# Reordering one stage of a fused two-block kernel: products, halves and second norm

## The chip, the cores and the metric

One core of one Trainium2 chip runs the whole program. The metric is device time in microseconds (us), the median of several executions. Five engines work side by side: TensorE (PE in the profile, PEld for its weight loads), VectorE (DVE), ScalarE (ACT), GpSimd (POOL) and SyncE (SP, which here only issues DMAs). Each engine takes its instructions strictly in the order written; they meet at semaphores.

## The reference, cut to what matters

The input is 16 sequences of 512 tokens and 128 features. Two blocks follow each other, and each normalises its input and adds the outputs of two branches to the unnormalised input:

```python
xn = layernorm(x);  x1 = x + scan_block(xn) + experts(xn)        # block 0
x1n = layernorm(x1); out = x1 + level_attention(x1n) + gated_cell(x1n)
# scan_block:  xi,z = split(xn@W_in); B,C = (xi@W_xp)@W_B, ..@W_C; h_t = a_t*h_(t-1) + B*xi
#              y = (C*h + D*xi) * silu(z);  return y @ W_out
# level_attention: W[t,s] = (Q_t.K_s) * decay(t,s) * lam[t, level(t,s)], lower triangle
#              o = (W@V) @ Wout.T + x;   return layernorm(o)*ln_g + ln_b
# gated_cell:  c = sigmoid(f)*c + sigmoid(i)*tanh(g) over the 16 rows; out = tanh(x@wo + c@uo + bo)
```

## The kernel before

Time is cut into 17 stages. Stage (i, j) runs block 1 of sequence i and block 0 of sequence j = i + 1 interleaved; the first has only j = 0, the last only i = 15, and 14 of the stages (i = 1 to 14) are one hardware loop body. In a stage every engine has a list of its own, `stages(i, j)`, written out by hand: its order is the whole schedule. Sequence i is cut into four tiles of 128 tokens (n = 0 to 3) and the tiles into chunks of 32.

The attention of a tile is computed in two parts. Inside a chunk, `pair_scores(i, n)` (TensorE, line 544) makes Q.K into the PSUM bank P1[1]; `pair_levels(i, n)` (line 556) spreads the level weights `nodesT` into P1[2]; VectorE's `pair_weights(i, n)` (lines 1323, 1329, 1333) multiplies the decay in `pair` by the levels, adds `self_lam`, and multiplies by the scores; `chunk_values` (581), `own_heads` (1355) and `chunk_sums` (589) apply it to the values. Across chunks, `left_halves` (TensorE 512 to 516, copied by ScalarE at 918 into `rs`) sums keys and values of left halves, `node_matrices` (530, copied at 928 into `ms`) multiplies them by the head matrices, and `levels`, `level_sum` (1343, 1348) and `tile_sum` (1366) add them up. What feeds them on VectorE: `node_lams` (1256) writes `nodes`, `node_rows` (1265) transposes it into `nodesT`. ScalarE's `pair_decay` (906 and 908) makes the decay from the differences; `own_values` (894) copies values.

Block 0 of sequence j: `scan_c` is the two products with MC (line 394, into P0[2] and P0[0]); the second needs the bank that `scan_inputs` (VectorE 1161) empties, and waits for `bx0_ready`. `scans` (1168, then the products 1173) is the recurrence, `top1` (1126 to 1145) the expert choice, and `gate0` (1178, 1181, 1185) the gating, of which one half stands in tile 0 and one in tile 1.

The second norm belongs to the sequence before: `attention_out(i-1)` (1372) adds the skip, `stats2` and `rstd2` give mean and scale, `norm2(i-1)` (1088, four instructions from `ob` into `skip`) normalises. GpSimd then runs `finish(i-1)` (1546, 1549) into `res`, SP stores `res`, and after that store GpSimd runs `residual(i)` (1499) and `keep_skip(i)` (1541). GpSimd's list per stage is `pair_differences` (1516), `level_values` (1529), `own_level` (1507, writes `self_lam`), `finish(i-1)`, `residual(i)`, `keep_skip(i)`. In the last stage GpSimd, ScalarE and VectorE also run `end_sum`, `end_tanh` and `end_add` for the 16 sequences.

VectorE's middle of a stage before the change reads: `node_lams, scan_inputs, norm2(i-1), node_rows, scans, pair_weights(0), top1, own_heads(0), pair_weights(1), level_sum(0), tile_sum(0), gate0(0), own_heads(1), pair_weights(2), ...`.

Of the kernel before, what the change touches and what calls it, by code (L numbers as in the profile page):

```python
# [23 lines left out]
TILES = T // 128  # L24
# [40 lines left out]
def build(nc, x, weights, consts, out):  # L65
# [9 lines left out]
    with ExitStack() as ctx:  # L75
# [96 lines left out]
        rs = sb("rs", 2048)  # L172
        ms = sb("ms", 2048)
        nodes = ms
        yt, ytT, ob = rs[:, 0:T], rs[:, T:2 * T], rs[:, 2 * T:3 * T]

        tf, ti, tg = ms[:, 0:T], ms[:, T:2 * T], rs[:, 3 * T:4 * T]
        ym = sb("ym", 2 * 512)
# [139 lines left out]
        def _(pe):  # L318
# [73 lines left out]
            def project(j, bank, free, value, lhs, done):  # L392
                pe.wait_ge(R[free], value)
                pe.matmul(P0[bank][:, :], lhs, xnT[:, :], start=True, stop=True).then_inc(R[done], 1)  # L394
# [6 lines left out]
                project(j, 0, "delta_ready", j + 1, MB[:, 0:128], "b0_ps")  # L401
                project(j, 1, "xi0_ready", j + 1, MB[:, 128:256], "b1_ps")

            def scan_c(j):
                project(j, 2, "xi1_ready", j + 1, MC[:, 0:128], "c0_ps")
                project(j, 0, "bx0_ready", j + 1, MC[:, 128:256], "c1_ps")

            def gate_z(j, q):
                if q == 0:
# [212 lines left out]
            def stages(i, j):  # L622
                if j is None:
                    for n in range(3):
                        recurrence(i, j, n)
                if i is not None:
                    heads(i, 0, 4)
                if j is not None:
                    turn_x(j)
                if i is not None:  # L630
                    heads(i, 4, 6)
                    heads(i, 6, 7)
                    running_sums(i)
                    heads(i, 7, 8)
                if j is not None:
                    logits(j)
                if i is not None:
                    left_ends(i)
                    heads(i, 8, 12)
                else:  # L640
                    fold_heads(0, 5)
                if j is not None:
                    scan_x(j)
                else:
                    cell_out()
                if i is not None:
                    heads(i, 12, 14)
                if j is not None:
                    scan_b(j)
                if i is not None:  # L650
                    heads(i, 14, H)
                else:
                    fold_heads(5, 8)
                if j is not None:
                    scan_c(j)
                if i is not None:
                    pair_scores(i, 0)
                    left_halves(i)
                    pair_levels(i, 0)
                    node_matrices(i)  # L660
                    pair_scores(i, 1)
                    chunk_values(i, 0)
                    pair_levels(i, 1)
                    levels(i, 0)
                if j is not None:
                    gate_z(j, 0)
                if i is not None:
                    chunk_sums(i, 0)
                if j is not None:
                    gate_z(j, 1)  # L670
                if i is not None:
                    pair_scores(i, 2)
                    chunk_values(i, 1)
                    pair_levels(i, 2)
                    levels(i, 1)
                if j is not None:
                    gate_u(j, 0)
                if i is not None:
                    chunk_sums(i, 1)
                    pair_scores(i, 3)  # L680
                    chunk_values(i, 2)
                    pair_levels(i, 3)
                    levels(i, 2)
                if j is not None:
                    gate_u(j, 1)
                if i is not None:
                    chunk_sums(i, 2)
                if i is not None:
                    levels(i, 3)
                if j is not None:  # L690
                    out0(j)
                if i is not None:
                    chunk_values(i, 3)
                    if j is not None:
                        recurrence(i, j, 0)
                        recurrence(i, j, 1)
                if j is not None:
                    turn_x1(j)
                if i is not None:
                    chunk_sums(i, 3)  # L700
                    if j is not None:
                        recurrence(i, j, 2)
                    turn_out(i)
                if j is not None:
                    values(j)
                if i is not None:
                    project_out(i)
# [11 lines left out]
        def _(act):  # L719
# [180 lines left out]
                act.wait_ge(R["lev_neg"], i + 1)  # L900
                act.activation(e4[:, :], lev[:, :], ACT.Exp).then_inc(R["e4_ready"], 1)

            def pair_decay(i):

                act.wait_ge(R["diff_ready"], i + 1)
                act.activation(pair[:, :], pair[:, :], ACT.Abs).then_inc(R["diff_abs"], 1)
                act.wait_ge(R["diff_abs"], i + 1)
                act.activation(pair[:, :], pair[:, :], ACT.Exp, scale=-1.0).then_inc(R["decay_ready"], 1)

            def left_halves(i):  # L910
                if later(i):
                    act.wait_ge(R["m_ps"], 4 * i)
                if later(i):
                    act.wait_ge(R["n_ready"], i)
                for n in range(TILES):
                    cols = 384 if n == 3 else 512
                    act.wait_ge(R["r_ps"], 4 * i + n + 1)
                    act.activation(rs[:, 512 * n:512 * n + cols], P1[(3, 4, 0, 3)[n]][:, 0:cols], ACT.Copy)\  # L918
                        .then_inc(R["r_copied"], 1)
# [26 lines left out]
            def stages(i, j):  # L946
# [40 lines left out]
                    fold_heads(5, 8)  # L987
                if i is not None:
                    heads(i, 14, H)
                    pair_decay(i)  # L990
                    own_values(i)
                    left_halves(i)
                    node_matrices(i)
                gelus()
                if j is not None:
# [28 lines left out]
        def _(dve):  # L1024
# [342 lines left out]

            def attention_out(i):
                dve.wait_ge(R["wo_ps"], i + 1)
                if later(i):  # L1370
                    dve.wait_ge(R["n_ready"], i)
                dve.tensor_tensor(ob[:, :], P1[1][:, :], skip[:, :], ALU.add).then_inc(R["ob_ready"], 1)

            def stats2(i):
# [31 lines left out]
            def stages(i, j):  # L1406
# [21 lines left out]
                if i is not None:  # L1428
                    level_weights(i)
                    if later(i):  # L1430
                        stats2(i - 1)
                    node_lams(i)
                if j is not None:
                    scan_inputs(j)
                if i is not None:
                    if later(i):
                        norm2(i - 1)
                    node_rows(i)
                if j is not None:
                    scans(j)  # L1440
                else:
                    cell_out()
                if i is not None:
                    pair_weights(i, 0)
                if j is not None:
                    top1(j)
                if i is not None:
                    own_heads(i, 0)
                    pair_weights(i, 1)
                    level_sum(i, 0)  # L1450
                    tile_sum(i, 0)
                if j is not None:
# [226 lines left out]
```

## Time and profile before

| | |
|---|---|
| median of 3 runs | 1216.23 us (1215.4 to 1220.75) |
| the profiled execution | 1215.93 us, its span 1213.8 us |
| TensorE busy | 1091.7 us, 90% |
| VectorE busy | 1004.4 us, 83% |
| ScalarE busy | 691.8 us, 57% |
| GpSimd busy | 310.4 us, 26% |
| mean granted TensorE clock | 0.959 |

The profiled execution took 2.1 us more than its span; the span runs from the first to the last instruction. A loop stage takes about 71 us and repeats almost exactly, so a stretch of one stage can be read for all. A busy share over the span says which engines could be the bound; which one is, at a given place, is read from who waits there.

### The profile page before, as it was taken

What the parts mean: (1) busy time and instruction counts of PE and PEld (TensorE: products, weight loads), DVE (VectorE), ACT (ScalarE), POOL (GpSimd) and SP (SyncE); (2) the same over time, 40 slices, a digit from 0 to 9 for tenths busy, and PEclk for the clock granted to TensorE, in tenths of its full rate; (3) what the DMA queues carried; (4) which work ended last, traced back from release to release, by engine and by line L of the source; (5) the groups of instructions that cost most, each with busy time, mean ns of one, the idle gap of its engine ahead of it and who ended that gap; (6) DMA issues with size and microseconds to landing.
All of it is one profiled execution on the core that took longest, in us unless ns stands there. A gap on an engine that the chain in (4) does not pass through costs nothing.

```text
span 1213.8 us, 18006 instructions
## 1 busy us (share of the span) xinstructions
PE 1091.7 (90%) x5756; PEld 665.3 (55%) x5756; DVE 1004.4 (83%) x2141; ACT 691.8 (57%) x1366; POOL 310.4 (26%) x197
## 2 busy tenths in 40 slices
PE   5799989998998989899998989989898998989872
PEld 3455646555564655556465555646555564655641
DVE  4688897979979797997979799797979979797677
ACT  4483845738375573837557283755728375572761
POOL 0050320504114050411405041140504114050273
PEclk9899989899999999999899999999999999999885
DMA  3000000000000000000000000000000000001136
GB/s 133 9 9 10 1 18 9 17 9 0 17 9 17 9 17 9 0 17 9 17 9 17 9 0 17 9 17 9 17 9 0 17 9 17 9 17 54 67 101 203
DMA packets 32562, 28.64 MB, mean 24 GB/s; under 512 B 1568, under 2 KB 26144, under 8 KB 32288
## 3 DMA queue, kind: packets, MB, share of 16 engines
q1 hardware_dynamic: 32544, 28.42, 7.2%
q8 instruction: 9, 0.15, 0.0%
q14 instruction: 9, 0.07, 0.0%
HBM read 16.09 MB, written 12.32 MB: 23 GB/s over the span
## 4 chain that ended last, share of the span: by engine, by line
PE 45%; DVE 37%; issue 11%; ACT 5%; DMA 1%; DVEq 0%; ACTq 0%; SPq 0%; POOLq 0%; POOL 0%
DVE ms L1256 6%; PE p L581 4%; PE p L619 3%; DVE skip L1088 3%; PE p L544 3%; PE p L556 2%; PE p L570 2%; DVE pair L1329 2%; DVE nodesT L1265 2%; PE p L433 2%; PE p L394 2%; ACT vdw L849 2%; PE p L424 2%; DVE pair L1323 2%; DVE y L1168 2%
## 5 line engine op out<-in xcount | busy, mean ns | idle before, releaser
L1516 POOL TENSOR_TENSOR pair<-pair,cgt 128x2048 f32<-128x2048 f32 x16 | 58.4, 3647 | 772.5 <-DVE pair L1316 772.5
L858 ACT ACTIVATE gx<-p 128x512 f32<-128x512 f32 x256 | 143.4, 591 | 13.9 <-PE p L479 8.2
L477 PE MATMUL p<-x1Th,Gl 128*128 128x512 f32 x256 | 120.1, 469 | 4.0 <-ACT gx L858 4.0
L813 ACT ACTIVATE gelu<-p,bias_u 128x512 f32<-128x512 f32 x32 | 22.0, 687 | 151.3 <-PE p L424 151.3
L479 PE MATMUL p<-x1Th,Gh 128*128 128x512 f32 x256 | 102.1, 399 | 0.0
L478 PE MATMUL p<-x1Tl,Gh 128*128 128x512 f32 x256 | 101.8, 398 | 0.0
L1529 POOL TENSOR_TENSOR vp<-vdw,beta 128x384 f32<-128x384 f32 (+3 forms) x80 | 80.9, 1042 | 56.0 <-DVE beta L1308 56.0
L544 PE MATMUL p<-gx,x1T 128*32 128x512 f32 x512 | 77.2, 679 | 12.8 <-DVE pair L1333 12.0
L581 PEld LDWEIGHTS p<-vbd,pair 128*128 128x128 f32 x512 | 62.0, 191 | 42.9 <-issue 31.0
L1256 DVE TENSOR_TENSOR ms<-lam,K 128x64 f32<-128x64 f32 (+4 forms) x80 | 84.5, 1132 | 0.0
L394 PE MATMUL p<-xnT,MC 128*128 128x512 f32 x64 | 42.6, 756 | 46.4 <-DVE y L1161 46.4
L581 PE MATMUL p<-vbd,pair 128*128 128x128 f32 x512 | 74.1, 288 | 1.5 <-DVE pair L1333 1.5
L1507 POOL TENSOR_TENSOR self_lam<-lam,K 128x2048 f32<-128x2048 f32 x16 | 75.0, 4689 | 0.0
L819 ACT ACTIVATE sm<-mv 128x4 f32<-128x4 f32 x32 | 6.6, 205 | 117.7 <-DVE mv L1083 117.7
L556 PE MATMUL p<-nodesT,K 128*128 128x512 f32 x128 | 66.7, 603 | 0.8 <-DVE nodesT L1265 0.8
L928 ACT ACTIVATE ms<-p 128x120 f32<-128x120 f32 x256 | 48.6, 276 | 30.1 <-PE p L530 24.6
L530 PEld LDWEIGHTS p<-rs,GT 128*128 128x128 f32 x512 | 60.1, 195 | 9.1 <-ACT rs L918 7.7
L516 PE MATMUL p<-vp,xn 128*128 128x384 f32 (+1 forms) x128 | 62.0, 607 | 3.1 <-ACT rs L918 3.1
L394 PE MATMUL p<-xnT,W 128*128 128x512 f32 x128 | 64.3, 606 | 0.0
L530 PE MATMUL p<-rs,GT 128*128 128x120 f32 x512 | 60.8, 278 | 0.0
L918 ACT ACTIVATE rs<-p 128x512 f32<-128x512 f32 x64 | 35.9, 570 | 43.0 <-PE p L516 40.1
L477 PEld LDWEIGHTS p<-x1Th,Gl 128*128 128x128 f32 x256 | 48.9, 191 | 19.3 <-ACT gx L858 8.0
(239 smaller groups left out, 2705.3 us busy)
## 6 DMA issues: line engine op xcount, KB each, us to landing
xin<-in_x SPq DMA_DIRECT2D x16, 256.0 KB, 2.8
hx_scratch<-vdw SPq DMA_DIRECT2D x16, 256.0 KB, 2.5
res_scratch<-res SPq DMA_DIRECT2D x15, 256.0 KB, 2.0
W<-in_weights SPq DMA_DIRECT2D x1, 1477.5 KB, 9.3
gx<-hx_scratch SPq DMA_DIRECT2D x5, 256.0 KB, 4.5
out<-gx SPq DMA_DIRECT2D x5, 256.0 KB, 2.7
gx<-in_weights SPq DMA_DIRECT2D x1, 1216.0 KB, 11.7
GT<-hx_scratch SPq DMA_DIRECT2D x4, 256.0 KB, 4.1
```

The costliest lines, as they stand in the source:

```text
L394: pe.matmul(P0[bank][:, :], lhs, xnT[:, :], start=True, stop=True).then_inc(R[done], 1)
L477: pe.matmul(head_bank(h)[:, :], tile(Gl, h), x1Th[:, :], start=True, stop=False)
L478: pe.matmul(head_bank(h)[:, :], tile(Gh, h), x1Tl[:, :], start=False, stop=False)
L479: pe.matmul(head_bank(h)[:, :], tile(Gh, h), x1Th[:, :], start=False, stop=True).then_inc(R["gx_ps"], 1)
L530: mm = pe.matmul(bank[:, 120 * a:120 * a + 120], tile(GT, h), view(rs[:, 0:1920], "p (n c) -> p n c", c=128)[:, :, HD * h:HD * h + HD], st ...
L544: mm = pe.matmul(P1[1][32 * c:32 * c + 32, :], x1T[:, 128 * n + 32 * c:128 * n + 32 * c + 32], view(gx[:, :], "p (h t) -> p h t", h=H)[:, ...
L556: pe.matmul(P1[2][:, :], k("left"), tile(nodesT, n, 512), start=True, stop=True).then_inc(R["lam_ps"], 1)
L581: mm = pe.matmul(tile(P1[3], g), pair[:, at:at + 128], vbd[:, at:at + 128], start=True, stop=True)
L858: act.activation(tile(gx, h, T), head_bank(h)[:, :], ACT.Copy).then_inc(R["gx_copied"], 1)
L1256: last = dve.tensor_tensor(nd[:, :, at:at + count], spread(l[:, :, level:level + 1], [128, 64, count]), spread(k("right", at, at + count). ...
L1507: pool.tensor_tensor(view(self_lam[:, :], "p (m t) -> p m t", t=CHUNK), spread(view(lam[:, :], "p (m l) -> p m l", l=LEVELS)[:, :, 0:1], [ ...
L1529: last = pool.tensor_tensor(view(vp[:, at:at + 128 * count], "p (s h e) -> p s h e", s=count, e=HD), spread(v.unsqueeze(1), [128, count, H ...
```

## The change

Four things move, and one buffer. TensorE runs the second MC product after `pair_scores(0)`, `left_halves` and `pair_levels(0)` instead of ahead of them. ScalarE splits `pair_decay` into its Abs (`pair_distance`) and its Exp, copies two left halves between the two, two after, and runs `own_values` after all four. VectorE runs `node_rows` ahead of `scan_inputs`, and `pair_weights(0)` ahead of `scans`; `norm2(i-1)` leaves its place after `scan_inputs` and stands after `pair_weights(1)`. The attention's output `ob` is no longer a quarter of `rs` but `skip` itself, added to and normalised in place; so `left_halves` waits for `ob_ready` and `c_ready` in place of `n_ready`, and `attention_out` for `skip_ready`.

```diff
-        yt, ytT, ob = rs[:, 0:T], rs[:, T:2 * T], rs[:, 2 * T:3 * T]
+        yt, ytT, ob = rs[:, 0:T], rs[:, T:2 * T], skip
...
-            def scan_c(j):
-                project(j, 2, "xi1_ready", j + 1, MC[:, 0:128], "c0_ps")
-                project(j, 0, "bx0_ready", j + 1, MC[:, 128:256], "c1_ps")
+            def scan_c(j, q):
+                if q == 0:
+                    project(j, 2, "xi1_ready", j + 1, MC[:, 0:128], "c0_ps")
+                else:
+                    project(j, 0, "bx0_ready", j + 1, MC[:, 128:256], "c1_ps")
...
                 if j is not None:
-                    scan_c(j)
+                    scan_c(j, 0)
                 if i is not None:
                     pair_scores(i, 0)
                     left_halves(i)
                     pair_levels(i, 0)
+                if j is not None:
+                    scan_c(j, 1)
+                if i is not None:
                     node_matrices(i)
                     pair_scores(i, 1)
...
-            def pair_decay(i):
+            def pair_distance(i):
 
                 act.wait_ge(R["diff_ready"], i + 1)
                 act.activation(pair[:, :], pair[:, :], ACT.Abs).then_inc(R["diff_abs"], 1)
+
+            def pair_decay(i):
+
                 act.wait_ge(R["diff_abs"], i + 1)
                 act.activation(pair[:, :], pair[:, :], ACT.Exp, scale=-1.0).then_inc(R["decay_ready"], 1)
 
-            def left_halves(i):
-                if later(i):
+            def left_halves(i, a, b):
+                if a == 0 and later(i):
                     act.wait_ge(R["m_ps"], 4 * i)
-                if later(i):
-                    act.wait_ge(R["n_ready"], i)
-                for n in range(TILES):
+                    act.wait_ge(R["ob_ready"], i)
+                    act.wait_ge(R["c_ready"], B if isinstance(i, int) else i)
+                for n in range(a, b):
...
                     heads(i, 14, H)
+                    pair_distance(i)
+                    left_halves(i, 0, 2)
                     pair_decay(i)
+                    left_halves(i, 2, TILES)
                     own_values(i)
-                    left_halves(i)
                     node_matrices(i)
...
                 dve.wait_ge(R["wo_ps"], i + 1)
-                if later(i):
-                    dve.wait_ge(R["n_ready"], i)
+                dve.wait_ge(R["skip_ready"], i + 1)
                 dve.tensor_tensor(ob[:, :], P1[1][:, :], skip[:, :], ALU.add).then_inc(R["ob_ready"], 1)
...
                     node_lams(i)
+                    node_rows(i)
                 if j is not None:
                     scan_inputs(j)
                 if i is not None:
-                    if later(i):
-                        norm2(i - 1)
-                    node_rows(i)
+                    pair_weights(i, 0)
                 if j is not None:
                     scans(j)
                 else:
                     cell_out()
-                if i is not None:
-                    pair_weights(i, 0)
                 if j is not None:
                     top1(j)
                 if i is not None:
                     own_heads(i, 0)
                     pair_weights(i, 1)
+                    if later(i):
+                        norm2(i - 1)
                     level_sum(i, 0)
                     tile_sum(i, 0)
```

## Rows read from the trace of the kernel before

**Rows 1.** The page, part 1: busy time, share and instructions of each engine.

```profile
PE 1091.7 (90%) x5756; PEld 665.3 (55%) x5756; DVE 1004.4 (83%) x2141; ACT 691.8 (57%) x1366; POOL 310.4 (26%) x197
```

**Rows 2.** The waits over the whole span: who waited for whom, total, times, longest.

```profile
PE p L394 <- DVE y L1161: 46.4, 15, 6.7
```

**Rows 3.** Timeline, TensorE, one loop stage: start, length, instruction, count, idle before.

```profile
507.54 1.02 PE L394 MATMUL p<-xnT,MC 128*128 128x512 f32 x2
511.53 1.13 PE L394 MATMUL p<-xnT,MC 128*128 128x512 f32 x2 [2.96 <-DVE y L1161]
...
514.99 2.31 PE L516 MATMUL p<-vp,xn 128*128 128x384 f32 x6
...
529.72 1.07 PE L544 MATMUL p<-gx,x1T 128*32 128x512 f32 x8
...
535.66 1.07 PE L544 MATMUL p<-gx,x1T 128*32 128x512 f32 x8 [0.19 <-DVE pair L1333]
```

**Rows 4.** Windows: busy of each engine, granted clock, DMA share, GB/s.

```profile
535.60:547.40 11.80, 11.74 (x84) 7.75 (x84) 8.94 (x17) 2.27 (x3) 0.00 (x0) 1.00 0.00 0
582.40:588.40 6.00, 5.96 (x14) 1.77 (x15) 6.00 (x7) 2.99 (x5) 4.99 (x3) 0.50 0.00 0
```

**Rows 5.** Timeline, VectorE, the same stage.

```profile
510.80 1.27 DVE L1161 TENSOR_TENSOR y<-p,xi 128x512 f32<-128x512 f32 x2
...
512.00 3.34 DVE L1088 TENSOR_SCALAR skip<-rs,mv,sm 128x128 f32<-128x128 f32 x4
...
515.26 2.30 DVE L1265 STREAM_TRANSPOSE nodesT<-ms 128x2048 f32<-128x2048 f32 x1
...
517.49 2.75 DVE L1168 TENSOR_TENSOR_SCAN y<-decay,y 128x512 f32<-128x512 f32 x2
...
521.34 0.67 DVE L1323 TENSOR_TENSOR pair<-pair,p 128x512 f32<-128x512 f32 x1
...
526.88 0.67 DVE L1355 TENSOR_TENSOR ym<-p,K 128x512 f32<-128x512 f32 x1
...
529.58 0.42 DVE L1343 TENSOR_TENSOR lv<-p,alpha 128x256 f32<-128x256 f32 x1
...
531.36 0.74 DVE L1181 SCALAR_TENSOR_TENSOR y<-xi,W,y 128x512 f32<-128x512 f32 x1
...
534.12 0.69 DVE L1329 TENSOR_TENSOR pair<-pair,self_lam 128x512 f32<-128x512 f32 x1
```

**Rows 6.** Timeline, GpSimd, the same stage.

```profile
509.69 4.80 POOL L1507 TENSOR_TENSOR self_lam<-lam,K 128x2048 f32<-128x2048 f32 x1
515.42 1.28 POOL L1546 TENSOR_TENSOR skip<-skip,W 128x512 f32<-128x512 f32 x1 [0.93 <-DVE skip L1088]
516.77 1.27 POOL L1549 TENSOR_TENSOR res<-res,skip 128x512 f32<-128x512 f32 x1
520.29 1.28 POOL L1499 TENSOR_TENSOR res<-x,W 128x512 f32<-128x512 f32 x1 [2.25 <-DMA res_scratch<-res]
```

**Rows 7.** Timeline, VectorE, stages 0 and 6, instructions beside a GpSimd one.

```profile
85.48 5.35 DVE L1168 TENSOR_TENSOR_SCAN y<-decay,y 128x512 f32<-128x512 f32 x2
...
499.21 2.37 DVE L1286 SCALAR_TENSOR_TENSOR lev<-lev 128x256 f32<-128x256 f32 x1
```

**Rows 8.** Timeline, ScalarE, the same stage as rows 3.

```profile
508.24 1.90 ACT L906 ACTIVATE pair<-pair 128x2048 f32<-128x2048 f32 x1
...
511.99 2.53 ACT L894 ACTIVATE vbd<-vdw 32x512 f32<-32x512 f32 x4
```

**Rows 9.** Windows: the first and last of eleven slow stretches, columns as rows 4.

```profile
226.70:233.60 6.90, 6.01 (x14) 1.82 (x15) 6.90 (x9) 3.86 (x5) 5.89 (x3) 0.51 0.00 0
...
1080.10:1083.50 3.40, 3.40 (x11) 0.71 (x10) 3.40 (x6) 2.43 (x5) 2.47 (x2) 0.50 0.00 0
```

**Rows 10.** Timeline, VectorE: the norm in the last stage and behind it.

```profile
1154.21 4.54 DVE L1088 TENSOR_SCALAR skip<-rs,mv,sm 128x128 f32<-128x128 f32 x4
...
1206.56 1.11 DVE L1088 TENSOR_SCALAR skip<-rs,mv,sm 128x128 f32<-128x128 f32 x4
```

## The prediction

> **What bounds the kernel now.** I read the busy table first [rows 1]: TensorE is busy for 90% of the span, VectorE for 83%, so either can be the bound, and each at its own place. The list of waits [rows 2] names the one large hole of TensorE: the second MC product waits for VectorE's `scan_inputs`, 46.4 us over 15 stages. The timeline of one loop stage shows it: the first product ends at 508.56, the second starts at 511.53, 2.96 us idle [rows 3]. VectorE has no gap there; it goes from `node_lams` into `scan_inputs` at 510.80, `norm2`, `node_rows`, `scans` and so on up to the tiles [rows 5]. So the first half of a stage is VectorE's. From `pair_scores(3)` at 535.66 on it is TensorE's: between 535.60 and 547.40 it is busy for 11.74 of 11.80 us and VectorE for 8.94 [rows 4]. In between, from `pair_scores(2)` at 529.72 to `pair_scores(3)` at 535.66 (5.94 us), both are full, TensorE idle for 0.19 us only [rows 3]. The date that decides is therefore that of `pair_scores(3)`: what is gained up to it goes through to the next stage, since all behind it hangs on TensorE.
>
> **The change, step by step.** I follow VectorE from 510.80 to that date, in the stage of [rows 3, 5, 6, 8].
>
> *Out of the old place:* `norm2` stood from 512.00 to 515.26, 3.26 us. Most of that is a stop: GpSimd's `own_level` runs beside it, from 509.69 to 514.49 [rows 6]. At the very end, where GpSimd is idle, the same four instructions took 1.11 us [rows 10], which is 1.03 until the next one starts (instructions overlap by 0.08 here, as 510.80 + 1.27 against 512.00 shows). In the new place GpSimd has nothing to do, its next work being `finish`, which waits for this very norm. So -3.26 and +1.03.
>
> *Scans:* from 517.49 to 521.34 the scans and the two products took 3.85 us [rows 5]. `finish` ran from 516.77 to 518.04 beside the first scan [rows 6]. That two-tensor instructions of VectorE stop for a GpSimd one is plain in stage 0, where the same two scans took 5.35 us instead of 2.75, and in the 256-element step at 499.21, 2.37 us [rows 7] where 256 elements take 0.42 in the row at 529.58 [rows 5]. I give back 0.44 us: a free scan of 1.12 us that starts at 517.49 would have ended the pair 0.44 earlier (the first ended about 1.08 after `finish`). -0.44.
>
> *A new wait ahead of `pair_weights(0)`:* `node_rows` now ends at 510.80 + 2.23 = 513.03, `scan_inputs` at 514.23. `pair_weights(0)` needs the decay and the level products. TensorE: `pair_scores(0)` ends near 509.6, `left_halves` may start when `level_values` is done (509.69, where `own_level` starts), and takes some 3.7 us (511.53 to 517.30 held one MC product, 1.06, one `pair_scores`, 1.0, and it), to 513.5; `pair_levels(0)` to 514.5. ScalarE: Abs until 510.14, two copies until 512.7, Exp 1.91 us until 514.6 [rows 8]. So VectorE waits 0.4 us. The second MC product then runs at 514.5, its input ready at 513.7: the 2.96 us hole is gone and the product is not late for `scans`. +0.4. `own_values` (2.53 us) is now behind the four copies, until 517.9; the node copies follow and end near 520.7, before `pair_scores(1)` is through. No cost.
>
> *Up to the tile:* `pair_weights(0)` and `top1` keep their 5.54 us (521.34 to 526.88). `own_heads(0)` comes at 526.88 - 3.26 - 0.44 + 0.4 = 523.6, and `pair_scores(2)` at 529.72 - 3.3 = 526.4; TensorE gets there at about 525.8. A lead of 3.3 us.
>
> *In the tiles:* the norm takes 1.03 us of it. What it sets free is the second cost. Let u be the start of `level_sum(0)`, 529.58 before and 527.3 now. `finish` starts 0.16 after u and runs 2.62 us to u+2.78 (515.42 to 518.04). The gate's step 1181, which reads two tensors from SBUF, stands at u+1.78 (531.36) and would be stopped until about u+2.78, ending 0.88 late (a stopped instruction ends by its own length less 0.12 after GpSimd's, as the scan does). Then the store: GpSimd's `residual` starts 2.25 us after `finish` (518.04 to 520.29), at u+5.03, until u+6.31; the step 1329 of `pair_weights(2)` (534.12) stands at u+4.54+0.88 = u+5.42 and is stopped too, +0.75. Together +1.63.
>
> Sum on VectorE: -3.26 - 0.44 + 0.4 + 1.03 + 1.63 = -0.64, say 0.65 us gained a stage, `pair_scores(3)` at 535.0. Over 14 stages 9.1 us. If neither collision happens it is 2.3 us a stage, if only the first 1.4; if VectorE's wait were 1 us longer the gain would be gone.
>
> The Trainium skill's page SBUF — State Buffer, section "SBUF: two separate sides", says the pair of ports that VectorE and GpSimd share is an exclusive lock held for the whole instruction, with two SBUF inputs enough to need it. The stage-0 scans above agree. By that rule a stopped instruction starts only when GpSimd's is wholly over, which would make each collision 0.12 us dearer and the stage's gain 0.4 instead of 0.65.
>
> *TensorE's clock.* Where TensorE lost 2.96 us, the granted clock fell to the lower of its levels (1.2 of 2.4 GHz) behind it in eleven of the thirteen stages from i = 2 on, in three of them for 6.8 us, in eight for 3.4 us, of which the first and the last are shown [rows 9]. It cost next to nothing there, because VectorE was the bound: 6.00 of 6.00 us busy in the one at 582.40 [rows 4]. The change closes that hole but opens another: TensorE starts `pair_scores(2)` at 526.4, has 5.75 us of work (5.94 less 0.19) and waits for `pair_weights(2)` until 535.0, 8.6 us later: about 2.8 us idle, most of it in one piece ahead of `pair_scores(3)`, just where TensorE becomes the bound. A stretch of 3.4 us at half clock costs up to 1.7 us there; I take 1.5, the stretch seldom starting on the instant. The hole is a little shorter than the old one and in two pieces, so I take half of the stages: 7 x 1.5 = 10.5 us. Bounds: none, and 12 stages with three double ones, 12 x 1.5 + 3 x 1.7 = 23.
>
> *The ends.* In the last stage `norm2` is stopped for longest (4.54 us, [rows 10]) and that goes. But `finish(14)` and so the store of `res`, the last loads and `end_sum` come some 10 us later, with a chain of loads, tanh and adds behind them. I take 0, bounds 3.5 us either way (4.54 less the 1.03 that stays). The other edits cost nothing: `ob` in `skip` needs `keep_skip`, over long before the next `attention_out`; the store of hx, now queued on SP behind the later store of `res`, is wanted only at the next stage's start, some 20 us on.
>
> **Sum.** 1215.9 (profiled execution) - 9.1 + 10.5 + 0 = 1217.3; the median of runs stands 0.3 above that execution. I say 1217.
>
> **The rivals.**
> - *No drop of the clock* (the idle piece too short): 1215.9 - 9.1 = 1207 us. For it: the hole before was longer, and the drop missed two stages even so. Against: 2.5 us is not much less than 2.96.
> - *No or one collision*: if `finish` and the gate miss each other, or `residual` comes after step 1329 (0.39 us of margin), gain 1.4 to 2.3 a stage, the hole of TensorE shrinks below 2 us and the clock stays up: 1215.9 - 20 = 1196 down to 1215.9 - 32 = 1184. Against: the offsets repeat to 0.1 us over the stages.
> - *Slower: the clock falls in nearly every stage* at the new hole, as it did at the old: 1215.9 - 9.1 + 23 = 1230. It decides the sign once drops in the loop cost more than 9.1 us, six at 1.5, and makes it measurably slower from ten.
>
> **Chances.** A run of this kernel tells 0.5%, about 6 us, from no change. Forecast (both collisions, drops in about half the stages, 1211 to 1223) 0.38; no drop 0.27; fewer collisions 0.14; slower by the clock or by a wait that I have not seen 0.21. So faster by over 0.5% 0.40, within 0.5% 0.38, slower 0.22. The range must reach into the cases of both signs: 1197 to 1228, leaving out the lower part of the third case and the end of the fourth.
>
> **What would show it.** In the profile after: the wait of the second MC product on step 1161 gone; step 1088 into `skip` at about 1.1 us for four; the first scan at 1.2 us, not 1.6; step 1181 of tile 0 near 1.6 us and step 1329 of tile 2 near 1.45; TensorE's idle ahead of line 544 grown to over 2 us once a stage, with low-clock stretches behind it. I am wrong if VectorE is not the bound up to `pair_weights(2)`, if GpSimd's steps fall elsewhere, or if stages that shorten shift the drops' places.

## The result and the profile after

The changed kernel takes 1227.8 us (median of five runs, 1224.3 to 1229.3) beside 1216.2 for the kernel before (five runs, 1214.7 to 1220.8): ratio 1.0077, 95% interval 1.0048 to 1.0105. It is 0.8% slower. The prediction said 1217 with a range of 1197 to 1228. The median lies 0.2 us inside the upper end and the profiled execution, 1229.3 us with a span of 1227.1, outside it, so that it fell into the range is luck. Of the cases it is the slower rival that came, the clock that falls in nearly every stage. Stages are numbered by i below.

The busy table of after, to compare with [rows 1], has TensorE's matmuls at 6.6 us more and VectorE at 12.7 us less:

```profile
PE 1098.3 (89%) x5756; PEld 670.4 (55%) x5756; DVE 991.7 (81%) x2141; ACT 682.8 (56%) x1366; POOL 316.3 (26%) x197
```

The list of waits of after (who waited for whom, total, times, longest) no longer has the wait of [rows 2] among the larger ones. In its place stands one of `pair_scores` (line 546 here) for the masked pair of `pair_weights` (line 1343):

```profile
PE p L546 <- DVE pair L1343: 45.0, 32, 2.4
```

The timeline of after, VectorE and TensorE, in the stage that answers to [rows 3, 5]. Lines 1171, 1333, 1178, 1098, 1353, 1191 and 1339 are the old 1161, 1323, 1168, 1088, 1343, 1181 and 1329; TensorE's 546 is the old 544:

```profile
515.67 3.43 DVE L1266 TENSOR_TENSOR ms<-lam,K 128x512 f32<-128x512 f32 x2
521.36 1.25 DVE L1171 TENSOR_TENSOR y<-p,xi 128x512 f32<-128x512 f32 x2
522.52 1.02 PE L394 MATMUL p<-xnT,MC 128*128 128x512 f32 x2
522.84 0.69 DVE L1333 TENSOR_TENSOR pair<-pair,p 128x512 f32<-128x512 f32 x1 [0.22 <-ACT pair L916]
525.03 2.33 DVE L1178 TENSOR_TENSOR_SCAN y<-decay,y 128x512 f32<-128x512 f32 x2
534.52 1.11 DVE L1098 TENSOR_SCALAR skip<-skip,mv,sm 128x128 f32<-128x128 f32 x4
534.66 1.06 PE L546 MATMUL p<-gx,x1T 128*32 128x512 f32 x8 [0.63 <-DVE pair L1343]
535.54 0.42 DVE L1353 TENSOR_TENSOR lv<-p,alpha 128x256 f32<-128x256 f32 x1
537.32 1.57 DVE L1191 SCALAR_TENSOR_TENSOR y<-xi,W,y 128x512 f32<-128x512 f32 x1
540.43 0.43 PE L591 MATMUL p<-ym,K 128*32 128x128 f32 x8 [0.37 <-DVE ym L1365]
540.91 1.49 DVE L1339 TENSOR_TENSOR pair<-pair,self_lam 128x512 f32<-128x512 f32 x1
543.24 1.94 PE L546 MATMUL p<-gx,x1T 128*32 128x512 f32 x8 [2.39 <-DVE pair L1343]
```

TensorE no longer idles ahead of the second MC product (522.52). The norm is 1.11 us for four, the scans 2.33 for two. The two steps that were forecast to be stopped are: 1.57 us where 0.74 stood, 1.49 where 0.69 stood. Just ahead of `pair_scores(3)` (543.24) TensorE idles 2.39 us. And that `pair_scores(3)` takes 1.94 us of TensorE, where before it took 1.07 [rows 3].

GpSimd, same stage of after, beside which the two stops lie (537.07 to 538.34, and 540.58 to 541.85):

```profile
535.71 1.28 POOL L1554 TENSOR_TENSOR skip<-skip,W 128x512 f32<-128x512 f32 x1 [13.01 <-DVE skip L1098]
537.07 1.27 POOL L1557 TENSOR_TENSOR res<-res,skip 128x512 f32<-128x512 f32 x1
540.58 1.27 POOL L1507 TENSOR_TENSOR res<-x,W 128x512 f32<-128x512 f32 x1 [2.25 <-DMA res_scratch<-res]
```

Windows of after (columns as in rows 4): the low-clock stretch at the hole in three stages, the first, the one above and the last of thirteen, and the way from `pair_scores(3)` to `chunk_values(3)`:

```profile
256.20:259.60 3.40, 3.29 (x14) 1.62 (x15) 3.16 (x7) 0.00 (x0) 0.00 (x0) 0.50 0.00 0
542.90:546.30 3.40, 3.06 (x13) 1.40 (x14) 3.16 (x7) 0.00 (x0) 0.00 (x0) 0.50 0.00 0
543.24:556.39 13.15, 13.15 (x84) 8.33 (x84) 8.99 (x16) 1.97 (x2) 0.00 (x0) 0.88 0.00 0
1116.40:1119.80 3.40, 3.07 (x13) 1.41 (x14) 3.16 (x7) 0.00 (x0) 0.00 (x0) 0.50 0.00 0
```

The same way before, in the same view:

```profile
535.66:547.37 11.71, 11.71 (x84) 7.72 (x84) 8.88 (x16) 2.21 (x3) 0.00 (x0) 1.00 0.00 0
```

The same 84 matmuls, no idle time in either, and 1.44 us more, because 3.06 of those us (543.24 to 546.30) ran at the lower level.

Where the time went. The last step of `node_lams` ends at 515.67 + 3.43 = 519.10 (the first VectorE row above); the same row before is this:

```profile
507.45 3.42 DVE L1256 TENSOR_TENSOR ms<-lam,K 128x512 f32<-128x512 f32 x2
```

It ends at 510.87, so this stage of after lies 8.23 us later. `pair_scores(3)` therefore starts at 543.24 - 8.23 = 535.01 in dates of before, where it was 535.66: 0.65 us gained. The stage with its hole filled, below, says the same: 70.28 us against 70.92. Then come the 1.44 lost. A stage, counted from one `scan_inputs` to the next, is 71.69 us in the middle of after, and 70.9 before (71.3 to 71.4 in the three whose low stretch is 6.8 us long). From the second `scan_inputs` to the last it is 996.8 us before and 1005.4 after, 8.6 more. The spans differ by 13.4 us. Of the other 4.8, the time up to the second `scan_inputs` is 7.4 longer and that from the last one on 2.6 shorter; 2.3 of each is `node_rows`, which now stands ahead of `scan_inputs` and only changes sides. Most of what is left of the first lies in low-clock stretches of the set-up. The windows from the first `scan_inputs` to the second, of before, of after, and of the kernel of experiment 1, which shares the set-up of after:

```profile
30.42:82.06 51.64, 41.98 (x174) 26.27 (x172) 37.63 (x88) 30.02 (x55) 8.00 (x5) 0.93 0.04 11
```

```profile
31.59:89.48 57.89, 47.92 (x183) 28.81 (x182) 39.94 (x88) 31.02 (x55) 10.34 (x7) 0.85 0.03 10
```

```profile
29.65:83.66 54.01, 43.45 (x183) 26.70 (x182) 39.94 (x89) 31.02 (x55) 10.33 (x7) 0.94 0.04 10
```

Before and the kernel of experiment 1 have one low-clock stretch of 6.8 us there, after has one of 10.2 besides. The kernel of experiment 1 takes 54.0 us, which is the 51.6 of before and the 2.3 of `node_rows`; after takes 3.9 more. The kernel of experiment 4 that fills the hole of before has the second stretch too, with the old order, and takes 55.6, 4.0 more than before. So the second stretch costs about 4 us, it comes with either order, and this part of the difference is not the change's. The kernels below that build on after take 54.0 to 58.0 us for this way, those that build on before 51.9 to 55.6.

### The profile page after: what moved, and what is told of

Its sections match the earlier page's. It is cut to its first block, busy times and chain, and to the rows that moved or that the text cites. A ratio compares the mean times of both kernels' runs of the same rounds, so it can differ in the third digit from the quotient of the medians.

```text
span 1227.1 us, 18021 instructions
## 1 busy us (share of the span) xinstructions
PE 1098.3 (89%) x5756; PEld 670.4 (55%) x5756; DVE 991.7 (81%) x2141; ACT 682.8 (56%) x1366; POOL 316.3 (26%) x197
## 4 chain that ended last, share of the span: by engine, by line
PE 40%; DVE 32%; issue 12%; ACT 8%; POOL 5%; DMA 1%; DVEq 1%; ACTq 0%; POOLq 0%; SPq 0%
POOL vp L1537 5%; DVE pair L1339 4%; PE p L583 4%; PE p L621 3%; DVE pair L1333 2%; PE p L546 2%; ACT pair L916 2%; PE p L518 2%; PE p L435 2%; PE p L572 2%; ACT vdw L854 2%; DVE pair L1343 2%; DVE y L1191 2%; DVE ym L1365 2%; PE p L426 2%
## 5 line engine op out<-in xcount | busy, mean ns | idle before, releaser
L583 PEld LDWEIGHTS p<-vbd,pair 128*128 128x128 f32 x512 | 69.4, 211 | 53.7 <-issue 39.3
L583 PE MATMUL p<-vbd,pair 128*128 128x128 f32 x512 | 81.5, 307 | 1.6 <-DVE pair L1343 1.6
L1515 POOL TENSOR_TENSOR self_lam<-lam,K 128x2048 f32<-128x2048 f32 x16 | 75.1, 4696 | 0.0
L1554 POOL TENSOR_TENSOR skip<-skip,W 128x512 f32<-128x512 f32 x16 | 20.4, 1278 | 205.5 <-DVE skip L1098 205.5
L532 PE MATMUL p<-rs,GT 128*128 128x120 f32 x512 | 65.3, 281 | 6.1 <-ACT ms L936 3.8
L518 PE MATMUL p<-vp,xn 128*128 128x384 f32 (+1 forms) x128 | 55.0, 552 | 5.9 <-POOL vp L1537 5.9
L1339 DVE TENSOR_TENSOR pair<-pair,self_lam 128x512 f32<-128x512 f32 x64 | 55.5, 867 | 3.3
L480 PEld LDWEIGHTS p<-x1Tl,Gh 128*128 128x128 f32 x256 | 48.8, 191 | 14.9 <-issue 7.6
```

The costliest lines, as they stand in the source:

```text
L480: pe.matmul(head_bank(h)[:, :], tile(Gh, h), x1Tl[:, :], start=False, stop=False)
L518: pe.matmul(bank[:, 0:cols], tile(xn1, n), vp[:, at:at + cols], start=True, stop=True)\
L532: mm = pe.matmul(bank[:, 120 * a:120 * a + 120], tile(GT, h), view(rs[:, 0:1920], "p (n c) -> p n c", c=128)[:, :, HD * h:HD * h + HD], st ...
L583: mm = pe.matmul(tile(P1[3], g), pair[:, at:at + 128], vbd[:, at:at + 128], start=True, stop=True)
L1339: dve.tensor_tensor(tile(pair, n, 512), tile(pair, n, 512), tile(self_lam, n, 512), ALU.add)\
L1515: pool.tensor_tensor(view(self_lam[:, :], "p (m t) -> p m t", t=CHUNK), spread(view(lam[:, :], "p (m l) -> p m l", l=LEVELS)[:, :, 0:1], [ ...
```

## The experiments

My theory after the result: GpSimd's steps stop two VectorE steps in tiles 0 and 2, that opens TensorE's hole ahead of `pair_scores(3)`, the hole brings the granted clock down, and it comes down just where TensorE is the bound. The rivals: the hole costs by itself, not through the clock; or the new order costs, not the norm's place.

### 1. GpSimd's three steps on one column

From the second sequence on, the changed kernel with

```diff
-                pool.tensor_tensor(view(res[:, :], ...), view(x1[:, :], ...), spread(w("lnbias")...), ALU.add)
+                c = 1 if later(j) else T
+                pool.tensor_tensor(res[:, 0:c], x1[:, 0:c], x1[:, 0:c], ALU.add)
...
-                pool.tensor_tensor(res[:, :], res[:, :], skip[:, :], ALU.add)
+                pool.tensor_tensor(res[:, 0:1], res[:, 0:1], skip[:, 0:1], ALU.add)
```

and the copy and the product into `skip` cut alike ("millisecond" in the text on record is a slip for microsecond).

> The changed kernel, in which GpSimd's four instructions behind the second norm (the two of finish, residual, keep_skip) work on one column instead of 512 from the second sequence on; so the second norm's scale, the residual sum and the skip are left out of the output. Nothing else moves. Theory (stops at the shared port open the hole of TensorE, and the hole lowers its clock): the gate step of tile 0 back from 1.57 to 0.74 us, the adding step of tile 2 back from 1.49 to 0.69, the hole ahead of pair_scores(3) down from 2.39 to about 0.8 us, no low stretch there, a stage 71.7 - 1.6 - 1.45 = 68.6 us, the whole 1228 - 43 = 1185 us. Rival (the norm's own millisecond on VectorE or the new order opens the hole, not GpSimd): hole about 2.4 us and low clock as they are, 1225 us.

Measured: 1180.7 us (1179.0 to 1183.0), ratio 0.9704 (0.9677 to 0.9731). A stage is 68.65 us, and from stage 2 on no stretch of the loop has a low clock. Timeline of this kernel, the same place:

```profile
517.80 0.75 DVE L1191 SCALAR_TENSOR_TENSOR y<-xi,W,y 128x512 f32<-128x512 f32 x1
520.58 0.69 DVE L1339 TENSOR_TENSOR pair<-pair,self_lam 128x512 f32<-128x512 f32 x1
522.11 1.06 PE L546 MATMUL p<-gx,x1T 128*32 128x512 f32 x8 [1.21 <-DVE pair L1343]
```

With GpSimd out of the way both steps have their free length again, the hole is 1.21 us, and the product behind it runs at full clock: 3.04 us a stage less than after. Of these, 1.62 are the two stops, added up from the lengths (0.82 and 0.80), and 1.4 is left for the clock.

### 2. The hole filled with needless products

```diff
                     chunk_sums(i, 1)
+                    for _ in range(2):
+                        pe.matmul(P1[3][:, :], ident, x1T[:, :], start=True, stop=True)
                     pair_scores(i, 3)
```

> The changed kernel, with two needless matrix products of 512 columns (into a bank that is free then) put into TensorE's hole, behind chunk_sums(1) and ahead of the wait of pair_scores(3): about 2 of its 2.4 us. No wait is taken away, VectorE and GpSimd are as before. Theory (the low clock costs 1.45 us a stage): no low stretch in the loop, a stage 70.2 us, the whole 1228 - 14 x 1.45 = 1207 us. Rival (the low clock is hidden, as it was before the change; the loss sits elsewhere): a stage stays at 71.7 us, 1228.

Measured: 1211.0 us (1208.4 to 1213.5), ratio 0.994 (0.9921 to 0.9959). A stage is 70.28 us, and from stage 2 on none has a low clock. TensorE's timeline:

```profile
536.63 1.98 PE L686 MATMUL p<-x1T,K 128*128 128x512 f32 x4
539.10 1.06 PE L546 MATMUL p<-gx,x1T 128*32 128x512 f32 x8 [0.48 <-DVE pair L1345]
```

VectorE's row is untouched and its two stops are still there; what went is 71.69 - 70.28 = 1.41 us a stage, by giving TensorE more work in a time when it had none. So the hole costs nothing by itself, and the clock is what costs: the first rival is out. Here two needless products make the kernel 17 us faster.

### 3. The norm in other places

The rest of the change kept whole, `norm2` moved: in one kernel ahead of `pair_weights(0)`, in one behind `own_heads(2)`.

```diff
                     pair_weights(i, 1)
-                    if later(i):
-                        norm2(i - 1)
                     level_sum(i, 0)
...
                     own_heads(i, 2)
+                    if later(i):
+                        norm2(i - 1)
                     level_sum(i, 2)
```

> The changed kernel with norm2(i-1) moved once more, from behind pair_weights(1) to behind own_heads(2), where TensorE is the bound. Theory: up to pair_weights(2) VectorE saves the norm's 1.03 us and both stops, 1.63; pair_scores(3) comes 2.6 us earlier, the hole is gone and with it the low clock: a stage 71.7 - 2.6 - 1.45 = 67.6 us, 1228 - 14 x 4.05 = 1171 us. Rivals: level_sum(2), now 1 us later, holds levels(3) up (slack about 1 us), or residual, now some 6 us later, holds sum0 up: each 0.5 to 1 us a stage, 1178 to 1185; if the norm is not what delays pair_scores(3), 1228.

Measured: 1178.8 us (1177.7 to 1180.8), ratio 0.9683 (0.9656 to 0.971). It is 37.5 us faster than before, the fastest of this study, though 8 us above what I had written. A stage is 67.73 us, where 67.6 was forecast, so the 8 us are not in the middle of the loop: stage 1 gains only 2.2 us of the 4, and the way from the last `scan_inputs` on is 2.7 longer than in after (135.0 against 132.3). Timeline of this kernel:

```profile
519.32 1.06 PE L546 MATMUL p<-gx,x1T 128*32 128x512 f32 x8 [0.19 <-DVE pair L1343]
523.32 1.11 DVE L1098 TENSOR_SCALAR skip<-skip,mv,sm 128x128 f32<-128x128 f32 x4
524.51 1.27 POOL L1554 TENSOR_TENSOR skip<-skip,W 128x512 f32<-128x512 f32 x1 [23.09 <-DVE skip L1098]
526.22 1.46 DVE L1339 TENSOR_TENSOR pair<-pair,self_lam 128x512 f32<-128x512 f32 x1
```

`pair_scores(3)` (519.32) is over before the norm starts (523.32), so there is no hole but 0.19 us. The stop has not gone: step 1339, now that of tile 3, is again 1.46 us. It lies behind the last `pair_scores`, where VectorE has slack, and costs nothing that the stage shows. All of the new order is in this kernel, so the order isn't what costs: the second rival is out, as it is by the next kernel.

> The changed kernel with norm2(i-1) put back behind scan_inputs, now ahead of pair_weights(0); all the rest of the new order stays. Theory: own_level is nearly over when the norm starts, so it takes 1.1 to 1.4 us there, 0.4 of it in VectorE's new wait; finish then stops the adding step of pair_weights(0) and the first scan, residual a step of top1, some 2 us; nothing is stopped in the tiles. pair_scores(3) about 0.5 to 1 us earlier than now, the hole ahead of it under 1 us, no low stretch: a stage 69.5 to 70 us, 1190 to 1203 us. Rival (the reorder of pair_weights(0) and the MC product is itself what costs): 1225 or more.

Measured: 1198.7 us (1196.5 to 1204.5), ratio 0.9839 (0.981 to 0.9867). Stages alternate between 69.48 and 70.5 us; every second one has a low-clock stretch. Timeline of one of those:

```profile
512.51 1.09 DVE L1098 TENSOR_SCALAR skip<-skip,mv,sm 128x128 f32<-128x128 f32 x4
516.22 2.62 DVE L1178 TENSOR_TENSOR_SCAN y<-decay,y 128x512 f32<-128x512 f32 x2
524.36 0.43 PE L591 MATMUL p<-ym,K 128*32 128x128 f32 x8 [1.81 <-DVE ym L1365]
526.48 1.94 PE L546 MATMUL p<-gx,x1T 128*32 128x512 f32 x8 [0.63 <-DVE pair L1343]
```

Here the norm is free too. GpSimd stops the adding step of `pair_weights(0)` (1.21 us against 0.69), the scans a little (2.62 against 2.33) and one step of `top1`, as forecast, by less than the 2 us that were forecast for it. What I hadn't forecast is the hole of 1.81 us ahead of `chunk_sums(0)`, with 0.63 more ahead of `pair_scores(2)`; behind it the clock falls in every second stage. The time lies in the forecast range in spite of that.

### 4. The norm alone, and the kernel before with its hole filled

Built on the kernel before, with `ob` in `skip`, but all orders old: `norm2` behind `pair_weights(1)` as in the change, or behind `own_heads(2)`.

```diff
                     scan_inputs(j)
                 if i is not None:
-                    if later(i):
-                        norm2(i - 1)
                     node_rows(i)
...
                     pair_weights(i, 1)
+                    if later(i):
+                        norm2(i - 1)
                     level_sum(i, 0)
```

> The kernel before, with the norm's part of the change alone: ob in skip, norm2(i-1) behind pair_weights(1). The orders of TensorE and ScalarE and the rest of VectorE's stay as before. Theory: TensorE keeps its 2.96 us hole ahead of the second MC product, and with VectorE 2.8 us lighter the work behind that hole (MC product, scores, left halves, node matrices) becomes what own_heads(0) and pair_scores(2) wait for, so pair_scores(2) comes only about 1.6 us earlier; norm and both stops take that back, pair_scores(3) 0 to 0.2 us earlier, and the low clock behind the old hole now costs: a stage 70.8 to 72 us, 1215 to 1230 us. Rival (the reorder of products brings nothing, all of the 3.3 us lead came from taking the norm out): as the changed kernel, 1228, with its low stretch ahead of tile 3.

Measured: 1271.3 us (1267.4 to 1273.8), ratio 1.0444 (1.0407 to 1.0481), a clear miss: 41 us above the upper end. Stages are 75.1 us, with low stretches at both places. Windows and timeline of this kernel:

```profile
527.30:534.10 6.80, 6.04 (x14) 1.85 (x15) 6.80 (x8) 3.71 (x5) 3.71 (x1) 0.50 0.00 0
554.60:558.00 3.40, 3.02 (x13) 1.36 (x14) 3.16 (x7) 0.00 (x0) 0.00 (x1) 0.50 0.00 0
```

```profile
528.05 2.07 PE L394 MATMUL p<-xnT,MC 128*128 128x512 f32 x2 [2.96 <-DVE y L1162]
537.62 0.69 DVE L1324 TENSOR_TENSOR pair<-pair,p 128x512 f32<-128x512 f32 x1 [3.24 <-PE p L556]
554.98 1.93 PE L544 MATMUL p<-gx,x1T 128*32 128x512 f32 x8 [2.14 <-DVE pair L1334]
```

The old hole is still there (2.96 us), and 6.8 us at half clock stand behind it. Before, those were free, since VectorE was late anyway. Now VectorE has lost its norm there, and it is VectorE that waits 3.24 us for TensorE's level products (second row). So a stretch that cost nothing costs once the other engine is made faster; stages 2 and 3 of this kernel, with one stretch of 3.4 us each, take 72.4 us, 2.7 less.

> The kernel before, with ob in skip and norm2(i-1) behind own_heads(2); no reorder on TensorE and ScalarE, node_rows and pair_weights(0) where they were. Beside e3 (1178.8 us) it prices the reorder. Theory: up to pair_scores(3) TensorE is the bound behind its old hole, that date about 1.75 us earlier than before, less what the low clock behind the hole takes (up to 1.5): a stage 69.2 to 70.4 us, 1192 to 1209 us, so the reorder is worth 1 to 2 per cent once the norm is out of the way. Rival (moving the norm does it all): 1178 us as e3.

Measured: 1206.5 us (1203.8 to 1213.1), ratio 0.9915 (0.989 to 0.994). Windows, of one stage's length, of this kernel without a low clock and with one, and of the stretch behind the next hole:

```profile
298.80:367.20 68.40, 64.92 (x353) 40.14 (x353) 59.23 (x132) 41.72 (x84) 17.75 (x12) 1.00 0.04 12
505.60:575.70 70.10, 66.58 (x353) 40.66 (x353) 59.28 (x132) 41.78 (x84) 17.80 (x12) 0.97 0.03 11
575.30:578.70 3.40, 2.99 (x10) 0.70 (x10) 3.40 (x4) 3.36 (x5) 3.36 (x1) 0.50 0.00 0
```

TensorE's timeline at the hole of each of these two stages:

```profile
300.28 1.13 PE L394 MATMUL p<-xnT,MC 128*128 128x512 f32 x2 [2.96 <-DVE y L1162]
301.33 1.06 PE L544 MATMUL p<-gx,x1T 128*32 128x512 f32 x8
...
505.62 1.12 PE L394 MATMUL p<-xnT,MC 128*128 128x512 f32 x2 [2.96 <-DVE y L1162]
506.67 1.63 PE L544 MATMUL p<-gx,x1T 128*32 128x512 f32 x8
```

The same hole to 0.01 us is left alone in stages 2 to 5 (68.45 us each) and brings the clock down in all nine from the next on (69.86 to 70.1). Beside the fastest kernel (1178.8) this one lacks only the new order of TensorE, ScalarE and VectorE: with the norm out of the way, that order is worth 27.7 us. In the profiled executions the two kernels differ by 23.1 us between the second `scan_inputs` and the last. About 12 of these are the low stretches of this one (eight whole stages at 1.4 to 1.65 us), and 0.72 us a stage is the order itself (68.45 against 67.73). So half of what the order brings there is that it closes the hole behind which the clock fell.

The last of this kind is the kernel before with two needless products between the MC products:

```diff
                 project(j, 2, "xi1_ready", j + 1, MC[:, 0:128], "c0_ps")
+                for _ in range(2):
+                    pe.matmul(P1[1][:, :], ident, x1T[:, :], start=True, stop=True)
                 project(j, 0, "bx0_ready", j + 1, MC[:, 128:256], "c1_ps")
```

> The kernel before, with two needless products of 512 columns (into P1[1], free then) between the two MC products: about 2 of the 2.96 us hole are filled and the clock should stay up. Theory (there VectorE is the bound, so the low clock cost nothing or 0.4 us where the low stretch was double): a stage 70.87 us throughout, 1214 to 1217 us against 1216 to 1217. Rival (the low clock was not free before the change either): 1195 to 1205 us.

Measured: 1216.9 us (1211.7 to 1220.9), ratio 0.999 (0.9969 to 1.001). No low clock from stage 2 to the end of the loop, and no time gained: a stage stays at 70.92. Window of one stage's length:

```profile
368.90:439.80 70.90, 67.18 (x358) 40.80 (x357) 60.74 (x132) 41.65 (x84) 17.78 (x12) 1.00 0.03 11
```

So the low clock of before was free, as the prediction read from [rows 4], but for 0.4 to 0.5 us in each of the three stages where it lasted 6.8 us. The same cure gives 17 us in one kernel and nothing in the other.

### 5. Why in every stage?

One needless product in the hole instead of two (the diff of experiment 2 without its loop):

> The changed kernel with one needless product instead of two in the hole ahead of pair_scores(3), so that about 1.4 us of it stay idle in one piece. Theory: the clock stays up, as behind the 1.3 us waits of the kernel before, and the time is that of e2, 1211 us. If the low stretch comes at all with 1.4 us idle, it does so in some stages only and the time lies between 1211 and 1228; if it depends on the date in the stage and not on the hole, 1228.

Measured: 1212.6 us (1210.6 to 1217.0), ratio 0.9956 (0.9936 to 0.9975). The hole is 1.33 us now, and of the stages from 2 on one alone, stage 10, has a low stretch; it takes 71.90 us where the others take 70.27. TensorE's timeline in it:

```profile
815.92 1.90 PE L546 MATMUL p<-gx,x1T 128*32 128x512 f32 x8 [1.33 <-DVE pair L1344]
```

The low stretches of after lie 71.7 us apart, each 21.5 to 21.8 us after its stage's `scan_inputs`, and the stage is that long only because of them (70.28 without). So it might be that a low stretch places the next stage's hole where the clock falls again. I tested that by making the stage longer elsewhere, ahead of `out0`, with two, one and three needless products:

```diff
                     levels(i, 3)
+                    for _ in range(2):
+                        pe.matmul(P1[3][:, :], ident, x1T[:, :], start=True, stop=True)
                 if j is not None:
                     out0(j)
```

> The changed kernel with two needless products ahead of out0, where TensorE is the bound: the hole ahead of pair_scores(3) and its length are untouched, the stage is about 1.9 us longer. It asks why the low clock came in thirteen of fourteen stages and not in half. Theory: the low stretches fall on dates of the chip's own, and the stage of the changed kernel, 70.25 us without and 71.7 us with one, had just the length at which each brings the next hole to the same date again; with 72.2 and 73.6 us it has not, so some stages go free: low stretches in 6 to 10 of 14, time 1240 to 1248 us. Rival (a hole of 2.4 us always brings the low clock): in 13 or 14 stages, 73.6 us each, 1255 us.

Measured: 1260.5 us (1258.6 to 1264.3), ratio 1.0374 (1.035 to 1.0399). The clock fell in 14 of 14 stages, every third one for 6.8 us. The theory had 6 to 10; it missed.

> As e9 with one needless product ahead of out0 instead of two: a stage about 71.2 us without a low stretch, 72.7 with. A look at its low stretches only. Theory (the hole of 2.4 us always brings one): in all 14 loop stages. Rival (it depends on where the chip's own dates cut the hole, as in e6, where the same 2.96 us hole went free in four stages): some stages free.

Measured in one run: 1250.7 us. Low stretches in 14 of 14, six of them 6.8 us long, as the theory had it.

> As e9 with three needless products ahead of out0: a stage about 73.1 us without a low stretch, 74.6 with. Theory (always): all 14 loop stages low. Rival (dates cut the hole): some stages free.

Measured in one run: 1263.8 us. Low stretches in 10 of 14; stages 3, 6, 9 and 13 have none and take 72.8 us, against 74.4 for those with a stretch of 3.4 us. Here it is the rival that came. TensorE's timeline at the hole in the hit stage 4, then in two stages one after the other, 5 (hit, after its `pair_scores`) and 6 (free):

```profile
407.65 1.43 PE L546 MATMUL p<-gx,x1T 128*32 128x512 f32 x8 [2.39 <-DVE pair L1345]
...
482.10 1.06 PE L546 MATMUL p<-gx,x1T 128*32 128x512 f32 x8 [2.40 <-DVE pair L1345]
...
556.55 1.06 PE L546 MATMUL p<-gx,x1T 128*32 128x512 f32 x8 [2.39 <-DVE pair L1345]
```

and the windows behind the last two:

```profile
483.30:486.70 3.40, 3.40 (x12) 1.90 (x13) 2.78 (x5) 0.00 (x0) 0.00 (x0) 0.50 0.00 0
557.00:560.40 3.40, 3.40 (x26) 1.91 (x18) 3.19 (x6) 0.00 (x0) 0.00 (x0) 1.00 0.00 0
```

The same hole, the same work around it, and one is hit and the other isn't. As in the four free stages of the old order, the hole's length does not decide alone; that its date counts is likely, but only argued, since the date is what I know to differ. The kernel before shows a drift of this kind: in stages 3, 4 and 5 the low stretch starts 0.27, 1.07 and 1.88 us behind `scan_inputs`, stage 6 is spared, in stage 7 it lasts 6.8 us, and the same follows again from stage 8 on. That a hole of some 2.4 us at this place is hit in 13 to 14 stages of three kernels and 10 of a fourth is measured. Why these and not the others, is left open.

## Why the prediction was right and wrong

*VectorE's row, right.* Its sum was a gain of 0.65 us at `pair_scores(3)`; measured 0.65. Term by term: norm in the tile 1.11 us for four as forecast; the new wait ahead of `pair_weights(0)` 0.22 instead of 0.4; step 1181 stopped by 0.83 (forecast 0.88), step 1329 by 0.80 (0.75). Experiment 1 took the stops away and the steps went back to 0.75 and 0.69, so GpSimd is shown to be their cause.

*Between row and rule, the row.* The Trainium skill, page SBUF — State Buffer, section "SBUF: two separate sides", would have had each stopped step start after GpSimd's was wholly over, and so the gain at 0.4. GpSimd's second step of `finish` ends at 538.34 and VectorE's ends at 538.89, 0.55 later, though it takes 0.75 alone; with `residual` it is 541.85 and 542.40, 0.55 again where 0.69 is the free length. That the stopped instruction waits for GpSimd's to end agrees with the trace; that nothing of it overlaps doesn't, by 0.14 to 0.20 us.

*TensorE's hole, right in place and size.* Forecast some 2.8 us in two pieces, most in one ahead of `pair_scores(3)`; measured 2.39 and 0.37. The price of a low stretch was put at 1.5 us; measured 1.44 (window), 1.41 (experiment 2).

*The number of stages, wrong.* The step that failed is "I take half of the stages: 7 x 1.5 = 10.5 us". It is thirteen: 13 x 1.44 = 18.7 us. With that one term exchanged the sum is 1215.9 - 14 x 0.65 + 18.7 = 1225.5 us; the rest to the profiled 1229.3 is 3.8, which is of the ends, put at nothing with bounds of 3.5 either way: the second low-clock stretch of the set-up, worth about 4 us, of which the prediction had no term. What I had to go by was the hole before, hit in eleven of thirteen stages; I halved that because the new hole is a little shorter. There was no ground for it: a hole of 2.96 us in the old order with the late norm was spared four times, and one of 1.33 us was hit once. The row at hand, eleven of thirteen, would have given 1223 us.

*The rivals.* "No drop", 1207, is what experiment 2 gives: 1211, the stage at 70.28 us as that rival has it (70.9 less 0.65), most of the rest lying in the set-up, which has the second low-clock stretch there too. "Fewer collisions", 1184 to 1196, is experiment 1, where both collisions are gone (1180.7). The slower rival came, at 1230 forecast and 1227.8 measured. That its price was so near is partly luck: it took 23 us for the clock, with three double stretches, where thirteen single ones cost 18.7 and the ends gave the rest. The stated range left out the end of this very case, and the time fell 0.2 us inside it.

*What the change is worth.* Its two halves pull in opposite directions. With the norm behind `own_heads(2)`, the order alone gives 27.7 us (half of it by the clock), and the whole 37.5 against before; with the norm left behind `scan_inputs` (second kernel of experiment 3) the whole gives 17.5. Where the change puts the norm, the 37.5 are given back and 11.6 more: 1227.8 against 1178.8 is 49 us for the place of four instructions that take 1.1. Of the 3.96 us a stage between these two kernels (71.69 and 67.73), 1.4 are the clock (experiment 2); the other 2.5 agree with the norm's 1.03 and the two stops' 1.62 ahead of `pair_scores(3)`, 2.65 together.

## What to carry to other kernels

Ask of every instruction that is moved which other engine's work it sets free, and where that lands: the 1.1 us of norm brought 1.6 more through GpSimd's `finish` and `residual`, and behind `own_heads(2)` none that the stage shows. Ask of every hole of TensorE what stands behind it: where another engine is the bound a low clock is free, where TensorE is the bound it costs 1.4 us each time in the changed kernel and 1.0 to 1.65 in the others, and a change that speeds up the other engine turns the first kind into the second. When holes of such a size were hit in most stages, count on most, and try a needless product in the hole to learn what the clock costs.

## What the runs showed of the hardware

- TensorE's granted clock fell to the lower level (0.50) behind holes of 2.96, 2.4 (with 0.37 a little ahead), 2.14, 1.81 (with 0.63 behind it) and once 1.33 us, for 3.4 or 6.8 us; I had not expected that of the short ones. Holes of 1.21 us (experiment 1) and 1.25 us (before with its hole filled) did not bring it in the loop, nor did 1.33 us in the other stages.
- The same hole, to 0.01 us and with the same work around it, is hit in some stages and spared in others; which, often repeats with a period of one, two, three or, in before, five stages.
- The set-up, between the first two `scan_inputs`, varies by 4 us between kernels that share it: 54.0 us with one low-clock stretch of 6.8 us, 57.9 with one of 10.2 us besides.
- A VectorE step that reads two tensors from SBUF took 1.57 us instead of 0.74, or 1.49 instead of 0.69, beside a GpSimd instruction of 1.27 us, and ended 0.55 us after it.
